# Attention stage: later keys masked by a TensorE matmul, one plain maximum a piece, the second query half first

## The reference

```
q, k, v = (x @ W).reshape(B, T, H, Dh) for W in (Wq, Wk, Wv)
scores = einsum('bthd,bshd->bhts', q, k) * tril(ones(T, T))
attn = softmax(scores / T ** 0.5)
out = einsum('bhts,bshd->bthd', attn, v).reshape(B, T, H * Dh) @ Wo
```

## Time and profile before

| what | value |
|---|---|
| median of 3 runs | 2213.99 us (2212.3 to 2214.46) |
| profiled execution | 2221.23 us, span 2219.5 us |
| mean granted clock of TensorE | 0.939 |
| busy: PE, DVE, POOL, ACT | 1996.0, 1276.7, 867.5, 817.4 us |
| rough matmuls (L954) | 384, 145.8 us busy |
| masked maxima (L1249) | 256, 122.8 us busy, and as many accumulator reads, 35.5 us |
| plain maxima (L1251) | 128, 84.8 us busy |
| clears (L1277) | 24, 21.9 us busy |

### The profile page before, as it was taken

The page is one execution under the profiler, slowest core; times in us unless marked ns, Lnnn a source line. Parts: engine busy times, 40 slices in busy tenths (PEclk is TensorE's granted clock), DMA queues, the critical chain, the costliest instruction groups (busy, mean ns, idle before and its releaser), DMA issues. The chain is left out here.

```text
span 2219.5 us, 29901 instructions
## 1 busy us (share of the span) xinstructions
PE 1996.0 (90%) x8700; PEld 1249.6 (56%) x8701; DVE 1276.7 (58%) x2970; ACT 817.4 (37%) x1549; POOL 867.5 (39%) x684
## 2 busy tenths in 40 slices
PE   5899958898888789986779999999999999999987
PEld 5566635455554756654545555555566555555556
DVE  6322275777775722216656666666656666667525
ACT  2122244554555212223324444444523444444423
POOL 0344311231112034441115556555424555665631
PEclk9999968999899689996769999999999999999999
DMA  9111232232220811124141122222032222212101
GB/s 385 48 58 63 55 126 29 29 44 43 29 29 1 341 52 63 57 54 179 21 95 45 47 57 57 57 57 57 12 75 54 56 58 57 50 44 50 31 1 51
DMA packets 60570, 150.63 MB, mean 68 GB/s; under 512 B 12976, under 2 KB 18304, under 8 KB 58176
## 3 DMA queue, kind: packets, MB, share of 16 engines
q1 hardware_dynamic: 50208, 120.43, 20.6%
q0 software_dynamic: 9120, 24.92, 3.6%
q10 hardware_dynamic: 1152, 4.19, 0.5%
HBM read 68.95 MB, written 18.61 MB: 39 GB/s over the span
## 5 line engine op out<-in xcount | busy, mean ns | idle before, releaser
L1834 POOL TENSOR_TENSOR mla_PS<-mla_PS,mla_PT 128x1024 f32<-128x1024 f32 x192 | 458.4, 2388 | 200.2 <-ACT mla_PT L2120 198.8
L2263 DVE TENSOR_REDUCE mla_MXP<-PS 128x1 f32<-128x512 f32 x512 | 334.4, 687 | 199.7 <-PE PS L1915 197.5
L2120 ACT ACTIVATE mla_PT<-PS 128x512 f32<-128x512 f32 x512 | 293.5, 599 | 421.0 <-PE PS L1935 375.4
L1944 PE MATMUL PS<-mla_PT,mla_CN 128*64 128x512 f32 x1024 | 274.2, 614 | 0.0
L521 DVE COPY moe_HT<-PS 128x512 f32<-128x512 f32 x92 | 63.7, 692 | 307.0 <-PE PS L644 301.2
L1915 PE MATMUL PS<-mla_KH,mla_QH 113*128 113x512 f32 x512 | 199.2, 456 | 18.0 <-DMA mla_KL<-mla_SL 17.8
L675 POOL DMA_INDIRECT moe_XS<-rows_in,moe_GI x96 | 93.7, 976 | 307.5 <-PE PS L630 171.3
L1935 PE MATMUL PS<-mla_QH,mla_KH 113*128 113x512 f32 x512 | 210.3, 411 | 1.7 <-ACT mla_QH L2104 1.5
L1935 PE MATMUL PS<-mla_QL,mla_KH 113*128 113x512 f32 x512 | 201.8, 394 | 0.0
L1935 PE MATMUL PS<-mla_QH,mla_KL 113*128 113x512 f32 x512 | 201.7, 394 | 0.0
L1140 ACT ACTIVATE att_PT<-PS 128x1024 f32<-128x1024 f32 (+1 forms) x192 | 152.3, 812 | 95.2 <-PE PS L975 93.4
(11 more groups left out here) (297 smaller groups left out, 3192.4 us busy)
## 6 DMA issues: line engine op xcount, KB each, us to landing
W<-in_W_dram SPq DMA_DIRECT2D x16, 2048.0 KB, 28.0
mla_QH<-mla_SH SPq DMA_DIRECT2D x64, 128.0 KB, 2.4
mla_KH<-mla_SH SPq DMA_DIRECT2D x64, 128.0 KB, 2.4
mla_QL<-mla_SL SPq DMA_DIRECT2D x64, 128.0 KB, 2.5
mla_KL<-mla_SL SPq DMA_DIRECT2D x64, 128.0 KB, 2.4
mla_KH<-mla_SH SPq DMA_DIRECT2D x64, 96.0 KB, 2.4
mla_KL<-mla_SL SPq DMA_DIRECT2D x64, 96.0 KB, 2.4
sums_Y<-rows_out SPq DMA_DIRECT2D x9, 512.0 KB, 6.0
```

The costliest lines, as they stand in the source:

```text
L1834: pool.tensor_tensor(PS[:, :], PT[:, slot(0), :] if k == 1 else PS[:, :], PT[:, slot(k), :], ALU.add).then_inc(s_ps.handle, 1)
L1944: ins = pe.matmul(bank(6)[h * DKVL:(h + 1) * DKVL, :], CN[:, b, k, 0:DKVL], PT[:, slot(k), h * HB:(h + 1) * HB], start=(k == 0), stop=(k = ...
L2120: act.activation(PT[:, slot(k), h * HB:(h + 1) * HB], bank(st_bank(s, h))[:, :], ACT.Exp, scale=MLA_SCALE).then_inc(s_p.handle, 1)
L2263: dve.tensor_reduce(MXP[:, n // NPC, c, h, t:t + 1], bank(piece_bank(n))[:, :], AX_X, ALU.max).then_inc(s_mx.handle, 1)
```

## The change

The masked pieces get a matmul more: the identity times LATER, a tile that holds 0 where a key is seen and -1e30 where it is later, is accumulated into the last 128 columns of each head in the piece. DVE then takes one plain maximum for a whole piece, all heads at once. Pieces are dealt anew: 27 for the second half and 11 for the first, 38 a group, and the second query half comes first in a group (`HALF`). The slots of the chain (block maximum, transposes, copies), of the fillers, projections, output copies, sums and output rows move with it. The clears go from DVE to POOL. Output rows are projected in the order in which halves end (`row_tile`).

```diff
@@ pieces
-            if rest <= 2 * P:
-                out += [(t, whole, whole * HB, rest, (h, h + 2)) for h in range(2)]
+            if rest == P:
+                out.append((t, whole, whole * HB, rest, tuple(range(HG))))
+            elif rest == 2 * P:
+                out += [(t, whole, whole * HB, rest, (h, h + 1)) for h in range(0, HG, 2)]
...
+    HALF = (1, 0)
+    pieces = [(q,) + p for q in HALF for p in pieces_of_block(q)]
-    FROM = 8
-    per_slot = {s: 2 for s in range(FROM, NSL)} | {s: 1 for s in range(FROM + 4, FROM + 8)} | {s: 2 for s in range(6)}
+    FROM = 7
+    per_slot = {s: 2 for s in range(FROM, 20)} | {s: 1 for s in range(20, NSL)} | {s: 1 + s % 2 for s in range(4)} | {4: 1, 5: 1}
...
-    key_of = lambda kk: (0, kk) if kk < 4 else (1, kk - 4)
+    key_of = lambda kk: (1, kk) if kk < TB else (0, kk - TB)
-    FILL = (3, 6, 9, 13, 15, 22)
+    FILL = (3, 6, 10, 16, 18, 21)
@@ projected_at
-        return (G + 2, (18, 20).index(s)) if s in (18, 20) and G + 2 < NG else None
+        return (G + 2, (12, 14).index(s)) if s in (12, 14) and G + 2 < NG else None
@@ POOL (the same function leaves DVE, where it stood at slots 7 and 14)
+                def clear_max_rows(H, r):
+                    q = HALF[r]
...
+                    for e in range(2):
+                        pool.memset(f32(QT[max_row(e), H % 2, e:HG:2, q * HB:(q + 1) * HB]), 0.0).then_inc(s_zero.handle, 1)
+                    pool.wait_ge(s_zero.handle, s_zero.at(4 * (H - 2) + 2 * r + 2))
...
+                        if s in (3, 5) and 2 <= G + 1 < NG:
+                            clear_max_rows(G + 1, (3, 5).index(s))
@@ PE, rough_scores
                         if H == 0 and n == 0:
+                            pe.wait_ge(s_c.handle, s_c.at(3))
                             pe.wait_ge(s_first.handle, s_first.at(NROW))
-                        elif n == (NPC0 if H == 0 else 0):
+                        if n == 0:
                             pe.wait_ge(s_rows.handle, s_rows.at(NROW * (H + 1)))
...
+                        masked = k0 + w == (i + 1) * P
                         for m, h in enumerate(hs):
                             ins = pe.matmul(out[:, m, :], QT[:, H % 2, h, i * P:(i + 1) * P], KT[:, H % 2, h // 2, k0:k0 + w], start=(m == 0),
-                                            stop=(m == len(hs) - 1))
+                                            stop=(m == len(hs) - 1 and not masked))
+                        if masked:
+                            ins = pe.matmul(out[:, :, w - P:w], IDR[:, :], bcast(LATER[:, :], 1, len(hs)), start=False, stop=True)
@@ PE, ahead of the loop and in it
-                rough_scores(0, range(NPC0))
+                rough_scores(0, range(NPC1))
                 max_rows(0, 0)
-                rough_scores(0, range(NPC0, begin[0]))
...
-                        if s == 6:
+                        if s == 8:
                             max_rows(G, 1)
-                        if s == 17 and G + 1 < NG:
+                        if s == 22 and G + 1 < NG:
                             max_rows(G + 1, 0)
...
-                        if s == 11:
+                        if s == 19:
                             out_transposes(G, 0)
@@ DVE, maxima
-                        if k0 + w == (4 * q + t + 1) * P:
-                            seen = SEEN[:, HB - w:HB]
-                            for m, h in enumerate(hs):
-                                part = bank(n % 2)[:, m * w:(m + 1) * w]
-                                ins = dve.tensor_tensor_reduce(part, part, seen, 1.0, LEAST, ALU.mult, ALU.max, MX[:, q, c, h, t:t + 1])
-                        else:
-                            ins = dve.tensor_reduce(MX[:, q, c, hs[0], t:t + 1], bank(n % 2)[:, 0:w], AX_X, ALU.max)
+                        part = bank(n % 2)[:, 0:len(hs) * w].rearrange("p (h k) -> p h k", k=w)
+                        ins = dve.tensor_reduce(MX[:, q, c, hs[0]:hs[-1] + 1, t], part, AX_X, ALU.max)
@@ DVE, in the loop
-                        if s == 6:
+                        if s == 7:
                             block_max(G, 1)
+                        if s == 9:
                             max_copies(G, 1)
-                        if s == 16 and G + 1 < NG:
+                        if s == 21 and G + 1 < NG:
                             block_max(G + 1, 0)
-                        if s == 17 and G + 1 < NG:
+                        if s == 22 and G + 1 < NG:
                             max_copies(G + 1, 0)
...
-                        if s == 12:
+                        if s == 20:
                             sums(G, 0)
```

More of the change, by code:

```diff
@@ L55 @@
 NLAT = DQL + DKVL
-LEAST = -3.0e38
+LEAST, UNSEEN = -3.0e38, 1.0e30
 MLA_SCALE = float(HD1 + RD) ** -0.5
@@ L728, in pieces_of_block @@
         return out
-    pieces = [(q,) + p for q in range(2) for p in pieces_of_block(q)]
+    HALF = (1, 0)
+    pieces = [(q,) + p for q in HALF for p in pieces_of_block(q)]
     NPC = len(pieces)
-    NPC0 = sum(1 for p in pieces if p[0] == 0)
-    FROM = 8
-    per_slot = {s: 2 for s in range(FROM, NSL)} | {s: 1 for s in range(FROM + 4, FROM + 8)} | {s: 2 for s in range(6)}
-    assert sum(per_slot.values()) == NPC and sum(per_slot[s] for s in range(FROM, FROM + 8)) == NPC0
+    NPC1 = sum(1 for p in pieces if p[0] == 1)
+    FROM = 7
+    per_slot = {s: 2 for s in range(FROM, 20)} | {s: 1 for s in range(20, NSL)} | {s: 1 + s % 2 for s in range(4)} | {4: 1, 5: 1}
+    assert sum(per_slot.values()) == NPC and sum(per_slot[s] for s in range(FROM, 21)) == NPC1
     ordered = list(range(FROM, NSL)) + list(range(0, 6))
@@ L743, in pieces_at @@
         H = G + 1 if s >= FROM else G
+        if H == 0:
+            return H, list(range(NPC1 + 2 * s, min(NPC1 + 2 * s + 2, NPC)))
         return H, list(range(begin[s], begin[s] + per_slot[s])) if H < NG else []
-    key_of = lambda kk: (0, kk) if kk < 4 else (1, kk - 4)
+    key_of = lambda kk: (1, kk) if kk < TB else (0, kk - TB)
     def columns(q, j):
@@ L753, in cuts @@
     def cuts(slots):
-        return min(slots, TB) + max(0, slots - 2 * TB)
-    FILL = (3, 6, 9, 13, 15, 22)
+        return max(0, slots - TB)
+    FILL = (3, 6, 10, 16, 18, 21)
     second = [x for i in range(TB) for x in (("rows", i), ("values", i))]
@@ L759, in attention_stage @@
     filler = {(n // 6, FILL[n % 6]): x for n, x in enumerate(second)}
-    filler |= {(n // 6 + 2, FILL[n % 6]): ("later", n - 5) for n in range(5, 13)}
-    filler |= {(NG0 + n // 4, FILL[1 + n % 4]): x for n, x in enumerate(first_out)}
+    filler |= {(n // 6 + 2, FILL[n % 6]): ("later", n - 6) for n in range(6, 14)}
+    filler |= {(NG0 + n // 4, FILL[2 + n % 4]): x for n, x in enumerate(first_out)}
     assert len(filler) == 5 * TB
@@ L868, in later_parts, with out_rows @@
                     pool.tensor_tensor(D1[:, :, :], e0, bcast(g.C[:, C_CNT + 4 * q:C_CNT + 4 * q + 4], 2, HG), ALU.mult).then_inc(s_f1.handle, 1)
-                def out_rows(G, q):
-                    n = 2 * G + q
+                def clear_max_rows(H, r):
+                    q = HALF[r]
+                    pool.wait_ge(s_st.handle, s_st.at(NSL * (H - 1)))
+                    pool.wait_ge(s_nm.handle, s_nm.at(8 * (H - 1)))
+                    pool.wait_ge(s_f1.handle, s_f1.at(4 * (H - 1)))
+                    pool.wait_ge(s_xn.handle, s_xn.at(t))
+                    for e in range(2):
+                        pool.memset(f32(QT[max_row(e), H % 2, e:HG:2, q * HB:(q + 1) * HB]), 0.0).then_inc(s_zero.handle, 1)
+                    pool.wait_ge(s_zero.handle, s_zero.at(4 * (H - 2) + 2 * r + 2))
+                def out_rows(G, r):
+                    n, q = 2 * G + r, HALF[r]
                     hs = slice(G % NG0 * HG * DH0, (G % NG0 + 1) * HG * DH0)
@@ L943, in rough_scores @@
                         if H == 0 and n == 0:
+                            pe.wait_ge(s_c.handle, s_c.at(3))
                             pe.wait_ge(s_first.handle, s_first.at(NROW))
-                        elif n == (NPC0 if H == 0 else 0):
+                        if n == 0:
                             pe.wait_ge(s_rows.handle, s_rows.at(NROW * (H + 1)))
-                        if n in (0, NPC0) and H >= 2:
+                        if n in (0, NPC1) and H >= 2:
                             pe.wait_ge(s_zero.handle, s_zero.at(4 * (H - 2) + (2 if n == 0 else 4)))
@@ L968, in scores_of @@
                     pair = s % 2
[L969 to L970 removed]
+                    if s in (0, 2 * TB):
+                        pe.wait_ge(s_nm.handle, s_nm.at(4 * (2 * G + s // (2 * TB) + 1)))
                     if NSL * G + s >= 2:
@@ L994, in values_of, with out_transposes @@
                     ins.then_inc(s_v.handle, 1)
-                def out_transposes(G, q):
-                    n = 2 * G + q
+                def out_transposes(G, r):
+                    n = 2 * G + r
                     misc(s_f2, 2 * n + 2)
@@ L1006, in outrows_t @@
                     for k in range(KD):
```

(20 more changed lines are left out.)

50 lines of the change are left out of this document (26 added, 24 removed).

## The result

The changed kernel takes 2224.05 us (median of 5 runs, 2219.96 to 2224.34), the kernel before 2213.36 beside it: ratio 1.0041 [1.003, 1.0052], slower by 0.4%. Forecast was 2196, faster, with a range up to 2218. The profiled execution took 2219.96 us, with a span of 2218.2. Two executions far off the rest (2864.97 us of the kernel before, 3822.5 us of the run with the clears on DVE) are in no ratio.

The account below looks back on a forecast made before the run. PE was taken to bound the attention loop (busy 329 of 372 us), then DVE. Terms -20 - 17 - 10 + 22 + 0 + 3 + 4 = -18 us gave a median of 2196 us, range 2168 to 2218.

Parts of the forecast that it names:

- (f): Next group's row DMAs against the first rough piece at slot 7: cover just used up, +3 us (0 to 12).
- (b): Slow-clock stretch behind the slot 6 event: goes with the idle, -17 us (bounds 0 and -22).
- (a): Event of slot 6, PE idle around DVE's block maximum and the MISC bank: mostly goes, -20 us (0 to -24).
- (g): Start of the loop: second half first makes the first rough piece wait for later rows, +4 us (2 to 10).
- (e): Clears moved from DVE to POOL: 0; if the cover were gone, 2 us in six groups.
- (c): DVE's plain maxima: less DVE work only shortens PE's waits for pieces, -10 us (bounds nothing and 30).
- DVE near 205 us in the loop: Sign that the forecast is right: DVE busy time in the loop falls from 262 to about 205 us.
- (d): Mask matmuls added on PE, 22 a group: +22 us, between nothing and 58.
- masks at full price: Rival, slower: mask loads or drains stay open, (d) is 58, total +18, 2232 us; chance 0.08.
- the end of the group: Rival, slower: stall moves to slot 22's maxima, (a) and (b) return at seven of eight places, 2228 us; chance 0.10.
- PE waiting ... for rows at slot 7 in every group: Sign that the forecast is wrong: PE waits over 1.5 us for maxima at slot 22 or 0, or for these rows.

Follow-up runs that it names:

- The repairs of the rows: Changed kernel with rows placed by token halves from the third group on and the second group's pieces from slot 9: 2190.31 us, 0.9892 against the kernel before.
- the runs without masks: Kernel with both row repairs, without mask matmuls: plain maxima, later keys counted, 2178.87 us (0.9844); or the old multiply-and-maximum masking on DVE, 2188.21 us (0.9895).

## Why the prediction was wrong

*Step (f) failed: "So the cover is just used up ... I take +3 (0 to 12)".* The repairs of the rows give back 33 us (1.0041 to 0.9892). Three things in it were off.

- When the rows are there. I took 11.5 us into the group from the mean DMA share. The share told rightly when the DMA engines fall idle, 505.2; but PE waits for the landing, and that comes later. In the kernel before, the last DMA is issued at 500.14 and lands 6.6 us later, at 506.7: 12.9 into the group and 1.5 us after the engines stop. After the change the last one is issued at 411.17 and lands 7.9 us later, at 419.1, 13.9 into the group, and PE starts at 419.09. Windows view and that one DMA (from its line's view), before:

```profile
504.00:505.00 1.00, 0.00 (x0) 0.00 (x0) 0.97 (x5) 0.33 (x1) 0.41 (x1) 1.00 1.06 135
505.00:506.00 1.00, 0.51 (x4) 0.42 (x4) 0.35 (x3) 0.00 (x0) 0.00 (x0) 1.00 0.11 12
506.00:507.00 1.00, 0.12 (x2) 0.00 (x0) 0.81 (x2) 0.82 (x2) 0.00 (x0) 1.00 0.00 0
...
DMA to landing us min/median/max: 6.6/6.6/6.6
```

and after:

```profile
416.00:417.00 1.00, 0.12 (x1) 0.00 (x0) 0.00 (x0) 0.96 (x2) 0.00 (x0) 1.00 0.98 119
417.00:418.00 1.00, 0.00 (x0) 0.00 (x0) 0.00 (x0) 0.18 (x1) 0.00 (x0) 1.00 0.26 33
418.00:419.00 1.00, 0.00 (x0) 0.00 (x0) 0.00 (x0) 0.00 (x0) 0.00 (x0) 0.69 0.00 0
...
DMA to landing us min/median/max: 7.9/7.9/7.9
```

- The cover. I counted 11.7 us up to the first rough piece; in groups 2 to 7 PE gets there in 9.9 to 11.6 and starts it at 13.1 to 13.9. Every stall that the change takes out of slots 0 to 6 brings this piece earlier, and the rows do not follow. The first group, for which (f) had 2 us more, waits 6.1 us.
- What follows a stall. Step (b) had priced the slow clock behind the old stall at 17 us, and in (f) I gave none to a new one. Five of the seven new waits are followed by slow matmuls, as steps (a) and (b) had described for the old ones, so most of what they had won went back.

*The rest of the sum* was -21 us without (f); with the rows repaired the kernel runs at 0.9892, -24. The total was near, the parts less so:

- (a), (b), (g): the event of slot 6 is gone, slot 6 is 0.6 to 1.25 us long for 4.4 to 4.9, and the loop's clock is 0.98 once the rows are repaired. The new order with the clears on GpSimd and the old masking gives -23 where (a), (b), (e) and (g) said -33. What fills the ten is open; in that run PE waits 3.6 us for the second group's rows and 3.9 us, in two places, for GpSimd's cuts of later keys, a wait that the kernel before does not have. (g), forecast 4, is 1 to 6 us over the profiles of the changed kernel and its variants.
- (c): -11 measured between the runs without masks, -10 forecast. The sign that went with it, DVE near 205 us in the loop, failed: it is 222. The sums of the earlier trace rows count time twice, as an accumulator read (400.37 to 400.51) starts before the recorded end of its reduction (399.89 to 400.46).
- (d): 10.6 measured, 22 forecast: a follower starts 0.06 us behind a mask of 128 columns, where I had taken the 0.11 between two rough matmuls. That some masks also fall into waits is likely but not shown. The rival of masks at full price is out.
- (e): forecast 0, since GpSimd hides the clears. That holds, as no wait of PE in the loop is put down to a clear; but leaving DVE is worth 14 us in this order; I had booked it as relief of an engine that is off the path. What the clears cost DVE in the old order, at slots 7 and 14, was not tried.

*The rivals.* The stall did move, but to slot 7 and the rows, not to the end of the group (at most 0.5 us there). "PE waiting ... for rows at slot 7 in every group" stood among the signs that would prove the forecast wrong, and it is the sign that appeared; its price was not among the rivals.

## What to carry to other kernels

When a change shortens the work ahead of a consumer, work out anew when each of its inputs arrives, from the landing of the last DMA and not from the moment when the DMA engines fall idle; a transfer that was hidden by a stall comes to light when the stall goes. Price a new stall as the old one was priced, with the slow clock behind it. Here the repair was to place the rows earlier and use them later, and it turned 0.4% slower into 1.1% faster.

## What the runs showed of the hardware

- The twelve row DMAs of a group (128 KB each) are issued 0.63 us apart and fill all 16 DMA engines (share 1.02, 135 GB/s); the first lands 3.3 us after its issue, the last 7.9. The last landing comes 1.5 us (before) to 1.8 us (after, 417.3 to 419.1) later than the end of the engines' busy time.
- A wait of 3 us on PE was followed by 5.9 us at a granted clock of 0.50; the same wait filled with matmuls whose result is thrown away kept 1.00, and waits of 1.9 and 2.3 us left it at 1.00 too.
